# Four strided writes and one whole read in place of one whole write and four strided reads, in the block exchange of an attention phase

## The reference

```
x = x + cross_attention_single_head(layernorm(x), ctx)
x = x + lora_moe(layernorm(x), 4 experts, top 2)
q = rope(layernorm(x) @ wq)   # 32 heads of 128
k = rope(ctx @ wk), v = ctx @ wv   # 8 heads of 128, each shared by 4 query heads
attn = softmax(q k^T / sqrt(128) + mask)
x = x + (attn @ v) @ wo
x = x + lora_moe(layernorm(x), 8 experts, top 1)
```

## Time and profile before

| | |
|---|---|
| time, median of 3 runs | 1777.59 us (1765.16 to 1779.57) |
| time of the profiled execution | 1777.91 us |
| its span in the profile | 1776.1 us |
| PE busy | 1739.9 us (98%) |
| DVE, ACT, POOL busy | 1102.9, 735.6, 783.0 us |
| DMA | 291.55 MB, 164 GB/s over the span |
| steps of the exchange | 64 |

### The profile page before, as it was taken

The page is one execution under the profiler, slowest core; times in us unless marked ns, Lnnn a source line. Parts: engine busy times, 40 slices in busy tenths (PEclk is TensorE's granted clock), DMA queues, the critical chain, the costliest instruction groups (busy, mean ns, idle before and its releaser), DMA issues.

```text
span 1776.1 us, 26431 instructions
## 1 busy us (share of the span) xinstructions
PE 1739.9 (98%) x8904; PEld 1576.3 (89%) x8904; DVE 1102.9 (62%) x2116; ACT 735.6 (41%) x1532; POOL 783.0 (44%) x588
## 2 busy tenths in 40 slices
PE   7999999999999999999999999999999999999998
PEld 6999999999888888888999999889989999999876
DVE  7631275566433333336666668898888988888845
ACT  5211210012333233222111023487788888878724
POOL 3223522125422222201222234487777787777724
PEclk9999999999999999999999999999999999999999
DMA  4112342235643333423433335799999999899843
GB/s 135 66 51 83 133 132 85 84 104 162 206 128 121 114 111 117 127 82 99 127 108 89 111 108 163 203 291 265 263 286 278 286 264 276 268 274 278 243 134 111
DMA packets 186402, 291.55 MB, mean 164 GB/s; under 512 B 48336, under 2 KB 146896, under 8 KB 185280
## 3 DMA queue, kind: packets, MB, share of 16 engines
q1 hardware_dynamic: 186304, 290.33, 54.6%
HBM read 193.01 MB, written 97.26 MB: 163 GB/s over the span
## 4 chain that ended last, share of the span: by engine, by line
PE 56%; DMA 20%; SPq 6%; DVE 3%; issue 2%; ACT 1%; POOL 1%; DVEq 0%; ACTq 0%; POOLq 0%
PE bank L200 52%; DMA probabilities<-q_rotated_then_x_rows 17%; SPq L1761 4%; SPq L1886 1%; PE bank L106 1%; PE bank L2328 1%; PE bank L186 1%; PE bank L2341 1%; DVE e_scores L1696 1%; POOL shared_operand_low L324 1%; DMA aw_weights_then_ctx_rows<-in_wk 0%; DVE q_rotated_then_x_rows L1739 0%; DVE e_p_t_low L1993 0%; DMA e_raw_then_a<-q_rotated 0%; POOL w_rest_low L789 0%
## 5 line engine op out<-in xcount | busy, mean ns | idle before, releaser
L200 PE MATMUL bank<-shared_operand_high,w_first_high 128*128 128x448 f32 (+1 forms) x768 | 279.1, 363 | 1.6 <-DVEq L805 0.7
L200 PE MATMUL bank<-shared_operand_low,w_first_high 128*128 128x448 f32 (+1 forms) x768 | 278.4, 363 | 0.0
L200 PE MATMUL bank<-shared_operand_high,w_first_low 128*128 128x448 f32 (+1 forms) x768 | 278.3, 362 | 0.0
L324 POOL TENSOR_TENSOR shared_operand_low<-ctx_raw,shared_operand_high 128x768 fp32r<-128x768 f32 x64 | 119.4, 1877 | 197.4 <-ACT shared_operand_high L320 197.3
L1452 POOL TENSOR_TENSOR w_first_low<-aw_weights_then_ctx_rows,w_first_high 128x1024 fp32r<-128x1024 f32 x30 | 72.1, 2402 | 221.7 <-ACT w_first_high L1420 221.7
L1704 ACT ACTIVATE e_scores<-e_scores,e_least 128x375 f32<-128x375 f32 x256 | 152.5, 597 | 18.7 <-DVE e_least L1696 17.9
L200 PEld LDWEIGHTS bank<-shared_operand_high,w_first_high 128*128 128x128 f32 x768 | 144.7, 188 | 13.2 <-POOL w_first_low L496 1.0
L200 PEld LDWEIGHTS bank<-shared_operand_high,w_first_low 128*128 128x128 f32 x768 | 144.6, 188 | 11.4
L200 PEld LDWEIGHTS bank<-shared_operand_low,w_first_high 128*128 128x128 f32 x768 | 144.7, 188 | 11.1
L320 ACT ACTIVATE shared_operand_high<-ctx_raw 128x768 fp32r<-128x768 f32 x64 | 52.8, 843 | 209.4 <-DMA ctx_raw<-in_ctx_t 190.9
L1696 DVE CUSTOM_DVE_ANT_0 e_scores<-bank,e_mask_then_layer_ffn 128x375 f32<-128x375 f32 x256 | 134.6, 528 | 0.0
(11 more groups left out here) (259 smaller groups left out, 4542.8 us busy)
## 6 DMA issues: line engine op xcount, KB each, us to landing
probabilities<-q_rotated_then_x_rows SPq DMA_DIRECT2D x64, 768.0 KB, 6.4
ctx_raw<-in_ctx_t SPq DMA_DIRECT2D x64, 384.0 KB, 3.9
e_shuffled_then_xn_t<-probabilities SPq DMA_DIRECT2D x128, 192.0 KB, 3.8
e_shuffled<-probabilities SPq DMA_DIRECT2D x128, 192.0 KB, 3.9
e_raw_wo<-in_wo SPq DMA_DIRECT2D x64, 256.0 KB, 5.1
aw_weights_then_ctx_rows<-in_wq SPq DMA_DIRECT2D x30, 512.0 KB, 3.8
q_rotated<-q_rotated_then_x_rows SPq DMA_DIRECT2D x64, 224.0 KB, 2.3
e_raw_then_a<-q_rotated SPq DMA_DIRECT2D x64, 224.0 KB, 6.6
```

What stands on the lines that cost most here:

```text
L200: mm = pe.matmul(out, stationary[a], moving[b], start=(first and i == 0), stop=(last and i == 2))
L324: pool.tensor_tensor(k.ctx_ring[1][slot][:, 2 * j:2 * j + 2, :], k.c_raw[:, j % 2], f32(k.ctx_ring[0][slot][:, 2 * j:2 * j + 2, :]), ALU.s ...
```

## The change

The data that is exchanged, its size and its place in the order of steps stay. What changes is which side of the trip does the regrouping. Before, `carry_out` is one transfer: each partition's 6144 bytes go to one run of 6144 bytes in DRAM; `carry_in` is four transfers, one for each block j of 32 partitions, each of which collects 4 x 32 pieces of 1536 bytes. After, `carry_out` is four transfers, one for each slice j of all 128 partitions, which place 4 x 32 pieces of 1536 bytes in DRAM in the order in which they are read; `carry_in` is one transfer of 128 runs of 6144 bytes. The semaphores' numbers follow: `carried` counts 64 for a step in place of 16, `shuffled` 16 in place of 64.

```diff
-    p_dram = nc.dram_tensor("probabilities", (2, P, BLOCKS, PER_GROUP * KEY_TILES * BLOCK), F32, kind="Internal").ap()
+    p_dram = nc.dram_tensor("probabilities", (2, BLOCKS, BLOCK, BLOCKS, PER_GROUP * KEY_TILES * BLOCK), F32, kind="Internal").ap()
...
-                dve.wait_ge(self.shuffled[t], 64 * (s // 2))
+                dve.wait_ge(self.shuffled[t], 16 * (s // 2))
...
         sp.wait_ge(self.transposed, 2 * s + 2)
         if s >= 2:
-            sp.wait_ge(self.shuffled[t], 64 * (s // 2))
-        sp.dma_start(self.k.p_dram[t], self.in_blocks[:, t]).then_inc(self.carried, 16)
+            sp.wait_ge(self.shuffled[t], 16 * (s // 2))
+        for j in range(BLOCKS):
+            sp.dma_start(self.k.p_dram[t, j].rearrange("a i x -> i a x"),
+                         self.in_blocks[:, t, j]).then_inc(self.carried, 16)
...
-        sp.wait_ge(self.carried, 16 * s + 16)
+        sp.wait_ge(self.carried, 64 * s + 64)
         if s >= 2:
             sp.wait_ge(self.pt_low_first, s - 1)
             sp.wait_ge(self.pt_low, 2 * s - 2)
-        for j in range(BLOCKS):
-            sp.dma_start(self.pt_raw[t][BLOCK * j:BLOCK * (j + 1)],
-                         self.k.p_dram[t, :, j].rearrange("(i a) x -> a i x", i=BLOCKS)).then_inc(
-                self.shuffled[t], 16)
+        sp.dma_start(self.pt_raw[t], self.k.p_dram[t].rearrange("j a i x -> (j a) i x")).then_inc(self.shuffled[t], 16)
...
-            act.wait_ge(first.shuffled[s % 2], 64 * (s // 2) + 64)
+            act.wait_ge(first.shuffled[s % 2], 16 * (s // 2) + 16)
...
-                    sp.wait_ge(s, 64 * GROUPS * BATCH // 2)
+                    sp.wait_ge(s, 16 * GROUPS * BATCH // 2)
```

## The result

| | before | after |
|---|---|---|
| time, median | 1774.92 us (4 runs, 1765.16 to 1779.57) | 2069.87 us (4 runs, 2068.05 to 2073.02) |
| time of the profiled execution | 1777.91 us | 2070.27 us |
| its span | 1776.1 us | 2068.5 us |

The ratio is 1.167, 95% interval 1.162 to 1.173: the change makes the kernel slower by a sixth.

What follows compares the result with a forecast made beforehand. SP's queue loop through the store's landing was taken as the bound, DMA and PE close behind. Profiled 1777.9 us + 415 (6.8 us more for each of 61 steps) + 11 for the ends = 2204 us; range 2030 to 2460 us.

Steps and rivals of the forecast that it cites:

- The bound: Attention phase: SP's queue loop through the store's landing sets the step, 9.01 us; DMA engines and PE within 10%.
- The leading 4 decides: Changed store: slowest dimension 4 in DRAM leaves four engines carrying it, 300.8 kB each per step against 153.
- at the mean rate: Store on four engines: 19.5 GB/s each, the mean of 25.4 and 13.6, giving 10.1 us a step.
- The rest of the step: Step beside the store: read 1.9 us, other bytes 3.0 us, engines' idle gap 0.8 us.
- the gap of 0.8 us: Time per step in which DMA engines idle, from the wait on the landing; claimed to stay at 0.8 us.
- The issues: SP's loop: six issues before and six after, 0.43 us each either way, nothing gained.
- The ends: Outside the 61 periods: 8 us for stores of steps 0 and 1, half of 16 uncovered, plus 3 at the end: 11 us.
- the tail: End of the exchange: last store lands later, the following read is about 3 us shorter; 3 us net added.
- Shared path: Rival: engines on blocks 32 partitions apart share a way into SBUF; step 20.2 us, 2477 us total; chance 0.22.
- All 16 engines: Rival: all 16 engines carry the store, SP's loop no longer binds, PE does; 1770 us; chance 0.07.
- The clock: Rival: idle PE falls to half clock and binds at 17.8 us a step; 2323 us; chance 0.07.
- What the profile was to show: Steady phase signs: landing 10 to 14 us, period near 16, DMA share 0.4 to 0.45, PE busy about 56%.

Runs made afterwards that it cites:

- by block: Changed kernel with its four stores cut by block of 32 partitions (32x4x384) instead of by slice of all 128: 1765.73 us, ratio 0.991.
- by rows: Kernel before with only the store cut in four by slice, into DRAM rows with leading number 128; reads unchanged: 1782.18 us, ratio 1.000.
- the curve over the leading number: Transfers alone, no computation; 768 KB as four stores with slowest DRAM dimension 16, 8, 4, 2: 4.53, 6.92, 10.73, 18.31 us.
- the half dose: Changed kernel with slices 0 and 1 stored as changed, slices 2 and 3 by block of 32 partitions: 1908.51 us, ratio 1.074.
- the last experiment: Transfers alone, no computation; 192 KB stores by four engines from partitions 0 to 3; 0, 4, 8, 12; 0, 32, 64, 96: 8.77, 3.52, 5.34 us.
- the extra PE work: Changed kernel with 14 more products of 448 columns on PE in each step from the fifth on: 2076.85 us, ratio 1.169.

## Why the prediction was right, and where its size was off

**The bound.** It was SP's loop through the landing of the store, as read: the chain shows the same loop after, and every experiment that gave the engines back (by block, by rows) gave the period back. What fills the loop now is the four engines' work, for they are seldom idle.

**The leading 4 decides.** Right, and shown five ways: the packet counts, the DMA share of 0.26 to 0.27 under a store, the curve over the leading number, the one change to 32x4x384, and the half dose. The Trainium skill's rule for the number of engines ("DMA: Bandwidth & Descriptors", section "Why a DMA increments its semaphore by 16 and not by 1") gave the right count: 4 for 4x32x384 against 128. The traces agree with it for the other forms too, with shares of 1.00 for leading 16 and 0.53 for leading 8, and by the packet counts.

**The size.** The forecast of 2204 us is 134 us over the measured 2070. The term that was mis-sized is the store, 10.1 us "at the mean rate" of 19.5 GB/s. The isolated transfers give 25.9 GB/s for an engine, and the stretches under a store in the kernel itself about 25, so 7.6 us (7.9 at 25); the 2.5 us between 10.1 and 7.6 make 152 us over 61 steps. The rest of the step was forecast at 1.9 + 3.0 + 0.8 = 5.7 us and comes out, as a remainder, at 13.6 - 7.6 = 6.0. The division inside it isn't measured, but the gap of 0.8 us was too large: the time with fewer than four engines at work is 0.4 us of a step. The prediction had the better value among its bounds (25.4 GB/s, a step of 13.4 us). It took the mean with the 13.6 GB/s of the four reads because the new store resembled both; the resemblance in run length was the false one, for runs of 1536 bytes go at full rate.

**The issues.** "0.43 us each either way" was not quite so: a store of the new form takes 0.51 to 0.52 us of SP when not held up. Of the four, three stand on the chain, ahead of the landing. From the issue of the read to the start of the landing it was 2.70 us in the step shown, against 2.32 before (1468.02 to 1470.34), 0.4 us more in each step, which the forecast has at nothing. The issue of query loads is held up behind the stores (1.92 us), without effect on the loop.

**The ends.** 8 us were forecast for steps 0 and 1. Of the 7.5 measured, 1.7 came before the first store of the exchange, so 5.8 are its own and the nearness is in part luck. SP was held 7.2 and 7.8 us longer there (1090.37 to 1101.80 and 1112.50 to 1124.02 us, against the earlier trace rows), as forecast; the half that was counted of it was a guess. For the tail 3 us were forecast and 5.1 measured. There the chain leaves the exchange: it goes through a load of values that queued 9.97 us behind the stores.

```profile
1977.17 9.97 DMA e_raw_then_a<-v_rows
```

**The rivals.** *Shared path*: it exists (the last experiment), but two engines that walk over the partitions in runs of 1536 bytes hardly suffer from it (10.87 against 10.54 us), and the four of the changed kernel move 25 GB/s each; a step of 20 us never came. What keeps them apart wasn't tried. *All 16 engines*: its result, 1770 us, is what the by-block kernel gave (1765.7), for the reason stated: PE binds. The changed kernel isn't that case. *The clock*: it did fall in part, to 0.87 over a stretch, and the extra PE work shows that it costs nothing that can be measured here. It explains most of why PE is busy for 77% of a stretch and not the 8.88 / 13.6 = 65% of its work at full clock: at 0.87 that work would fill 75%, by an estimate from these rows.

**What the profile was to show.** The landing of 10 to 14 us behind the last of the four stores came, at 10.3 to 11.5 in the four steps read. The read, to land in under 4 us, took 4.2 to 5.2, with a median of 4.3. The period was to be near 16 us and was 13.6; with it the DMA share came at 0.54 and not 0.40 to 0.45, GB/s at 183 and not 155, PE busy at 77% and not 56%. PE does wait for the probabilities' low parts, 104.7 us in all. The first 1088 us were not quite unchanged: the first store of the exchange is 1.7 us later, by 0.2%, ahead of all that was changed.

## What to carry to other kernels

Before a transfer is cut another way, look at the slowest dimension of both sides as the program carries it: 4 there confined it to four DMA engines, at some 25 to 26 GB/s each, though the tile had all 128 partitions. A low mean DMA share together with long landings is the sign. If regrouping has to be paid on one side, cut by blocks of partitions (32x4x384) and keep the side whose issues stand behind the wait as one transfer: that gained 0.9% here (interval 0.7% to 1.1%). Nor is a trip through DRAM the only way between blocks of partitions, as the description of the kernel has it: this kernel's own layernorm turns its tiles on PE (`norm_turn`, L101). Whether that would serve the probabilities wasn't tried.

## What the runs showed of the hardware

A transfer issued on SP's queue ran on 16 DMA engines where its slowest dimension was 128, 112, 32 or 16, and on 8, 4 or 2 where it was 8, 4 or 2 (by the packets under 512 bytes; the shares for 16, 8 and 4 agree, 1.00, 0.53 and 0.27). An engine moves 25.9 GB/s in runs of 1536 bytes (from leading 4 to 2), and about 25 in runs of 6144 (393 to 406 GB/s for 16). Around a store of 768 KB by 128 rows lie some 1.3 to 1.6 us (3.27 and 3.53 us against 1.9 for the data), around one with a leading 8, 4 or 2 it is 3.1 us.

Four partitions side by side share one path, and partitions 32 apart share it too: 27 to 28 GB/s by the differences of the stores, 35 by those of the loads. The Trainium skill's map ("SBUF — State Buffer", section "Door 1: The DMA port swizzle") agrees with which of the partitions tried share. Transfers by block of 32 partitions take longer than those of all 128: 4.76 us against 3.53 for a store, 5.50 against 4.20 for a load.
